# A decoder layer on one core: the context is split into two 16-bit parts first and transposed by DMA, instead of transposed on TensorE and split behind it

## What is computed

```python
src_trans = jnp.einsum('bsf,of->bso', src, W_src) + b_src       # src: the context, 8 x 512 x 1024
src_trans = src_trans * src_mask[:, :, None]
src_key, src_val = jnp.split(src_trans, 2, axis=2)              # keys and values of cross-attention
```

## Time and profile before

| | |
|---|---|
| median of three runs | 2157.06 us |
| the profiled execution, first to last instruction | 2153.7 us |
| TensorE busy | 1991.5 us (92%) |
| VectorE busy | 1472.0 us (68%) |
| ScalarE busy | 785.4 us (36%) |
| GpSimd busy | 179.0 us (8%) |
| context transposes on TensorE | 256 instructions, L567 |
| cT lo on VectorE | 64 instructions, 43.8 us |

### The profile page before, as it was taken

One profiled execution on the slowest core, in us unless ns is written; L12 is line 12 of the kernel. 1 busy time (PEld: TensorE's weight loads), 2 busy tenths in 40 slices (PEclk: granted clock), 3 DMA queues, 4 the chain that ended last, 5 costly groups with the idle time before them and its releaser, 6 DMA issues. The chain is left out here.

```text
span 2153.7 us, 35330 instructions
## 1 busy us (share of the span) xinstructions
PE 1991.5 (92%) x13100; PEld 1057.1 (49%) x13100; DVE 1472.0 (68%) x1762; ACT 785.4 (36%) x1209; POOL 179.0 (8%) x448
## 2 busy tenths in 40 slices
PE   6999898988899899956789999999999999999998
PEld 5555454544455445533454545545445454554543
DVE  4289997989898898898675556555565655656531
ACT  3322122122222122111574636536264462644622
POOL 0000002000010001053000010000100001000010
PEclk8999999999999899988899999999999999999999
DMA  6112221212111221312734041320413204141010
GB/s 207 40 50 59 74 65 49 69 60 64 64 59 58 70 74 50 110 52 83 179 111 104 2 95 50 64 80 1 100 44 81 64 1 109 35 95 30 1 40 20
DMA packets 151599, 143.35 MB, mean 67 GB/s; under 512 B 55529, under 2 KB 108777, under 8 KB 151426
## 3 DMA queue, kind: packets, MB, share of 16 engines
q1 hardware_dynamic: 147056, 140.58, 23.2%
q10 hardware_dynamic: 4370, 0.34, 0.2%
HBM read 94.75 MB, written 33.55 MB: 60 GB/s over the span
## 5 line engine op out<-in xcount | busy, mean ns | idle before, releaser
L1488 DVE TENSOR_TENSOR p_lo<-k,p_hi 128x1024 f16<-128x1024 f32 x128 | 156.8, 1225 | 193.8 <-ACT p_hi L1376 193.8
L888 DVE TENSOR_REDUCE ctx<-prod 128x512 f32<-128x4096 f32 (+1 forms) x32 | 215.3, 6728 | 0.1
L1177 PE MATMUL b_ff<-x2T_hi,w1T_hi 128*128 128x512 f16 x512 | 195.3, 381 | 2.3 <-DVE x2T_lo L1488 2.3
L1533 DVE CUSTOM_DVE_ANT_0 junk<-b_sx,mneg 128x512 f16<-128x512 f32 x256 | 175.7, 686 | 30.7 <-issue 22.3
L1177 PE MATMUL b_ff<-x2T_lo,w1T_hi 128*128 128x512 f16 x512 | 195.1, 381 | 0.0
L1177 PE MATMUL b_ff<-x2T_hi,w1T_lo 128*128 128x512 f16 x512 | 195.1, 381 | 0.0
L1408 ACT ACTIVATE k<-b_st,mbias 128x512 f32<-128x512 f32 x256 | 161.6, 684 | 14.2 <-PE b_st L1221 14.1
L604 PE MATMUL pj_b<-winT_hi,xT_hi 128*128 128x512 f16 x384 | 146.1, 380 | 6.3 <-DVE xT_lo L822 6.3
L1376 ACT ACTIVATE p_hi<-k 128x1024 f16<-128x1024 f32 x128 | 135.3, 1057 | 44.2 <-PE b_av L1236 41.9
L604 PE MATMUL pj_b<-winT_hi,xT_lo 128*128 128x512 f16 x384 | 145.5, 379 | 0.0
L604 PE MATMUL pj_b<-winT_lo,xT_hi 128*128 128x512 f16 x384 | 145.5, 379 | 0.0
(11 more groups left out here) (263 smaller groups left out, 4157.2 us busy)
## 6 DMA issues: line engine op xcount, KB each, us to landing
cn<-in_ctx_dram SPq DMA_DIRECT2D x64, 256.0 KB, 2.8
k<-kT_scratch SPq DMA_DIRECT2D x24, 512.0 KB, 7.9
xn<-in_x_dram SPq DMA_DIRECT2D x32, 256.0 KB, 2.9
xres<-in_x_dram SPq DMA_DIRECT2D x32, 256.0 KB, 3.0
x_scratch<-x SPq DMA_DIRECT2D x32, 256.0 KB, 2.0
q<-x_scratch SPq DMA_DIRECT2D x8, 1024.0 KB, 5.6
q<-x_scratch SPq DMA_DIRECT2D x32, 256.0 KB, 4.0
out_dram<-q SPq DMA_DIRECT2D x32, 256.0 KB, 4.5
```

What stands on the lines that cost most here:

```text
L888: dve.tensor_reduce(ctx1[:, cols], prod[:, :, cols].rearrange("p s e -> p e s"), AX.X, ALU.add).then_inc(s["av_done"], 1)
L1177: mm = pe.matmul(out, a, c, start=(start and n == 0), stop=end)
L1488: dve.tensor_tensor(dst, bank, hi, ALU.subtract).then_inc(out, 1)
L1533: dve.tensor_tensor_reduce(junk[:, :], sx_b[tt % 2][:, :], mneg[:, :], 1.0, NEG, ALU.add, ALU.max, mx[:, h % 2, tt:tt + 1]).then_inc(s["sx ...
```

## The change

The context quarter is split before it is transposed. ScalarE now copies the loaded rows `cn` to `cs_hi` (two buffers) in float16, GpSimd subtracts to get `cs_lo` (one buffer), and SyncE issues two DMA transposes, 128 x 512 float16 each, from these to cT hi and cT lo. TensorE's transposes of the context, the bank `st_b` and VectorE's `context_lo` are gone. Each of the two orders by hand keeps its places; the load of a quarter is issued one quarter earlier in the queue's count (off + 6 in place of off + 5), behind the two transposes of off + 4.

```diff
             def load_context(b, off):
-                wait_from(sp, s["st_filled"], 16 * b + off - 1)
+                wait_from(sp, s["c_lo"], 16 * b + off - 1)
...
+            def turn_context(b, off):
+
+                sp.wait_ge(s["c_lo"], 16 * b + off + 1)
+                stand_alone(sp, alone["sp"])
+                wait_from(sp, s["sm_filled"], 16 * b + off - off % 4 - 4)
+                stand_alone(sp, alone["sp"])
+                for z, src in enumerate((cs_hi[off % 2], cs_lo)):
+                    sp.dma_start_transpose(cT_part(z, off), src[:, :]).then_inc(c_turned[off % 2], 16)
...
             def s_phase(b, tail):                                  # SyncE
                 for t, offs in enumerate(S_QUARTERS):
                     for off in offs:
-                        load_context(b, off + 5)
+                        turn_context(b, off + 4)
+                        load_context(b, off + 6)
...
+            def context_lo(b, off):                                # GpSimd
+
+                pool.wait_ge(s["c_hi"], 16 * b + off + 1)
+                wait_from(pool, c_turned[(off - 1) % 2], 32 * (8 * b + (off + 1) // 2))
+                pool.tensor_tensor(cs_lo[:, :], cn[off % 2][:, :], cs_hi[off % 2][:, :],
+                                   ALU.subtract).then_inc(s["c_lo"], 1)
...
-            def context_transposes(b, off):                        # TensorE
-
-                wait_from(pe, s["st_lo"], 16 * b + off)
-                pe.wait_ge(cn_ld[off % 2], 16 * (8 * b + off // 2 + 1))
-                for j in range(4):
-                    mm = pe.transpose(st_b[:, j * P:(j + 1) * P], cn[off % 2][:, j * P:(j + 1) * P], w.ident[:, :])
-                mm.then_inc(s["st_filled"], 1)
...
                 if c == 0:                                         # TensorE, context_products
-                    pe.wait_ge(s["st_lo"], n + 4)
+                    for i in range(2):
+                        pe.wait_ge(c_turned[i], 64 * (4 * b + off // 4 + 1))
...
             def context_hi(b, off):                                # ScalarE
-                act.wait_ge(s["st_filled"], 16 * b + off + 1)
-                act.activation(cT_part(0, off), bank4(st_b), ACT.Copy).then_inc(s["st_hi"], 1)
+                act.wait_ge(cn_ld[off % 2], 16 * (8 * b + off // 2 + 1))
+                wait_from(act, c_turned[off % 2], 32 * (8 * b + off // 2))
+                act.activation(cs_hi[off % 2][:, :], cn[off % 2][:, :], ACT.Copy).then_inc(s["c_hi"], 1)
...
-            def context_lo(b, off):                                # VectorE
-                low(cT_part(1, off), bank4(st_b), cT_part(0, off), s["st_hi"], 16 * b + off + 1, s["st_lo"])
```

More of the change, by code:

```diff
@@ L313, in phase_a @@
     cn = [sb(f"cn{i}", [P, 512], F32) for i in range(2)]
+    cs_hi, cs_lo = [sb(f"cs_hi{i}", [P, 512], F16) for i in range(2)], sb("cs_lo", [P, 512], F16)
     cT = [pair(f"cT{i}", [P, CT, 256]) for i in range(2)]
@@ L372, in av_operands, with has_quarter @@
         return by_head(prod), probs, by_head(v)
-    def has_transposes(b, off):
-        return not (isinstance(b, int) and 16 * b + off + 4 >= QUARTERS)
+    def has_quarter(b, off):
+        return not (isinstance(b, int) and 16 * b + off >= QUARTERS)
     def bank4(bank):
@@ L456, in av_phase @@
                     for off in offs:
-                        if has_transposes(b, off + 1):
-                            load_context(b, off + 5)
+                        if has_quarter(b, off + 4):
+                            turn_context(b, off + 4)
+                        if has_quarter(b, off + 6):
+                            load_context(b, off + 6)
                     if t < T - 1:
@@ L463, in av_phase @@
                     for off in offs:
-                        if off % 4 == 2 and has_transposes(b, off - 2):
+                        if off % 4 == 2 and has_quarter(b, off + 2):
                             load_mask(b, off + 2)
@@ L477, in _ @@
                 load_x(0, t)
-            for off in range(2, 5):
-                load_context(0, off)
+            for off in range(4):
+                turn_context(0, off)
+                load_context(0, off + 2)
             s_phase(0, False)
@@ L537, in s_phase @@
                     for off in offs:
+                        context_lo(b, off + 4)
                         if off % 4 == 2:
@@ L551, in _ @@
             scale_mask(0, 0)
+            for off in range(4):
+                context_lo(0, off)
             s_phase(0, False)
@@ L763, in s_phase @@
                     for i, off in enumerate(offs):
[L764 to L765 removed]
+                        context_hi(b, off + 4)
                         if i == 0:
@@ L777, in av_phase @@
                     for off in offs:
-                        if has_transposes(b, off):
+                        if has_quarter(b, off + 4):
                             context_hi(b, off + 4)
@@ L919, in av_phase @@
                 last = isinstance(b, int) and b == NB - 1
-                def transposes_lo(t, offs):
-                    for off in offs:
-                        if has_transposes(b, off):
-                            context_lo(b, off + 4)
-                    if not last:
-                        x_lo(b + 1, t)
                 for t, offs in enumerate(AV_QUARTERS):
                     if t == 0:
-                        transposes_lo(0, offs)
+                        if not last:
+                            x_lo(b + 1, 0)
                         softmax(b)
                     context_products(b, t)
-                    if t < 2:
-                        transposes_lo(t + 1, AV_QUARTERS[t + 1])
-                    elif t > 2:
-                        transposes_lo(t, offs)
+                    if not last and t != 2:
+                        x_lo(b + 1, t + 1 if t < 2 else t)
                     if t >= 2:
```

17 lines of the change are left out of this document (3 added, 14 removed).

## The result

The changed kernel takes 2213.0 us (median of four runs, 2212.2 to 2219.0) against 2157.6 us for the kernel before in the same comparison: a ratio of 1.027, interval 1.025 to 1.029. It is slower by 55 us. The forecast was 2126.1 us, and the range of 2110 to 2200 doesn't hold the result.

A forecast was written before the change was run, and what follows sets the result against it. TensorE was taken to set the pace in the scores stages, VectorE or TensorE in the values stages. Span 2153.7 - 32.6 for the removal + 1.6 stall = 2122.7 us, 2126.1 with the 3.4 us around it; range 2110 to 2200.

The forecast's parts named there:

- The removal: Work taken off TensorE and VectorE in phase_a: 0.49 us a quarter where TensorE paces, 0.60 where VectorE does, 32.6 us.
- The window of 99 us: Stretch of the earlier trace taken as one scores stage, with TensorE busy for 96.5 us and VectorE for 84.7.
- The split: Gain by place: 2.0 us before the first stage, 19.6 scores stages, 4.4 and 5.4 values stages, 1.2 last block.
- The transposes' own time P: Time from issuing a pair of transposes on SyncE until both have landed: 3.6 to 15.8 us, taken as 4.8.
- slow transposes: Rival: long transposes make TensorE stand at a group's first product; middle 2175 us, far end 2225; chance 0.33.
- The subtraction on GpSimd: 64 subtractions moved to GpSimd, 1.5 us each and up to 5.9 beside a VectorE product, costed at nothing.
- The row of 4.28 us: Earlier GpSimd instruction on a single column, begun 0.16 us after a VectorE product of two SBUF operands; it ended with it.
- The cover named: On SyncE, a quarter's transposes must wait anyway for the previous quarter's stores, which wait for VectorE's sums; this hides GpSimd's subtraction.
- SyncE's queue: Loads standing behind the transposes on SyncE are used two quarters later, so their delay was given no cost.
- The first product of a group: TensorE's wait for all four context tiles; room 4.4, 8.4 and 7.4 us for off 4, 8, 12; stall 1.6 us.
- transposes that eat the gain: Rival: transposes of 9.2 to 10.0 us a pair, or VectorE waiting for GpSimd, cancel the gain; 2157 us, chance 0.09.
- row of 3.37 us: Earlier VectorE product begun while a GpSimd instruction ran, against 3.35 us for its group; cited against GpSimd holding up products.

The follow-up runs named there:

- e5_removal: The kernel before, without TensorE's transposes, ScalarE's copy and VectorE's subtraction of the context, and nothing in their place: 2127.0 us, ratio 0.986.
- e4_copies: The changed kernel with each DMA transpose replaced by a plain DMA copy of the same 128 KB: 2185.4 us, ratio 1.012 to the kernel before.
- e1_order: The changed kernel with GpSimd's context subtraction ahead of the normalisation factors in the scores stages: 2189.1 us, ratio 1.014 to the kernel before.
- e11_memset: e6_mask with GpSimd writing zeros in place of the subtraction, all waits and transposes kept: 2128.2 us, ratio 0.986 to the kernel before.
- e2_xload: The changed kernel with SyncE's x loads moved ahead of the transposes: 2179.7 us, ratio 1.011 to the kernel before.
- e3_both: The changed kernel with the edits of e1_order and e2_xload together: 2152.3 us, ratio 0.997 to the kernel before.
- e6_mask: e3_both with GpSimd scaling the mask one quarter later and SyncE loading it ahead of the transposes: 2147.7 us, ratio 0.996 to the kernel before.

## Why the prediction was wrong

**The removal: right.** 32.6 us forecast, 32 measured (e5_removal), and VectorE did not become the bound, but for the last values stage, which is 1.8 us longer (TensorE's wait for VectorE's sums there is 7.3 us, 1.1 before). The window of 99 us taken for the scores stage ends 4.5 us too early, which this sum doesn't use. The split was off: the four scores stages lost 27.7 us in all instead of 19.6, the values stages 6.0 instead of about 11, so that the total's fit to 1 us is partly luck.

**The transposes' own time P: right, a little high.** Forecast 4.8 us for a pair, from 3.6 to 15.8. Measured 1.25 for the first issue and 2.5 for the second's landing, 3.75 us in the median of the 64 pairs (8.1 at most). The rival "slow transposes", the only one that ended on the slower side, had the sign but not the mechanism: it needed a P above 9.6 us. The two prices that it turned on stand thus in the trace: landing takes 2.4 to 2.5 us, issuing 1.20 to 1.25 us where the earlier trace rows have 0.60 for a copy. The Trainium skill's Advanced Engine Details and Errata (X-Bar Transpose), by which a transposing DMA is as fast as a plain one, agrees with the trace nearly for the landing (2.5 against 2.3 us) and not for the issue. The estimate of 10.5 us from VectorE: DVE Perf Modes (The three transpose paths) is not borne out: the eight blocks of a pair took 3.75 us. P as defined also misses what a longer issue does to whatever stands behind it on SyncE, and that was worth 28 us in this order (e4_copies).

**The subtraction on GpSimd: right in size, wrong in its cover. This is the step that failed.** Forecast 1.5 us each, up to 5.9; measured 1.15 alone, 2.0 in the mean, up to 5.4. The row of 4.28 us in the earlier trace rows was read rightly, and the contention that it and the rule speak of is there. But the text asked only what stands *behind* the subtraction in GpSimd's order ("the factors are used two values steps later"). In the scores stages of the later blocks the factors stand *ahead* of it, and the very row shows in its bracket that GpSimd had waited 24.05 us for VectorE. The cover named, SyncE's stores that come no earlier, is no cover for a subtraction that begins 24 us after ScalarE's copy. Price: 24 us for the factors (e1_order). On top of it come 19.5 us for the subtraction as such (e11_memset; 0.5 us of writing is left in there), which the forecast had at nothing.

**SyncE's queue: the second step that failed.** "On SyncE the loads, which are used two quarters later" was the whole reckoning. It holds for the context's loads. The x loads stand in the same queue, and TensorE takes them at the start of a values stage. They now stand behind transposes that wait for GpSimd, and behind the loop's end, and came 3.4 to 8.9 us late in six places. Price: 33 us (e2_xload). The rival "transposes that eat the gain" looked at VectorE instead: its product with q and k takes 4.47 us in the mean, against 4.41 before. The prediction's ground for this, that GpSimd gives way, was half of the truth: its row of 3.37 us had an overlap of 0.15 us only, and two products that began 0.04 us behind a subtraction took 5.39 us. They were few, so it cost little.

**The first product of a group.** The stall was made of P less the room between SyncE's place and the product. The room was read rightly, but it is room only if the transposes are issued when SyncE reaches that place. They were issued when GpSimd had delivered: 12.4 us of wait at the second group, where 0.4 were forecast. With the order mended and the subtraction short (e11_memset) it is 1.0.

**The clock: no term at all.** The prediction counts waits alone. Where TensorE stood, its granted clock fell, from 0.97 to 0.88 in the scores stage, and the work behind the wait ran at the lower level. By the estimate above that is some 22 of the 94 us between e5_removal and the changed kernel in `phase_a`; the prices of 24, 33 and 19.5 us hold their share of it. No run changed the clock by itself.

**The sum.** In the measured terms: 2158.9 - 32 for the removal, + 61 for the two orders (24 and 33 singly), + 25 for what e3_both keeps above e5_removal, is 2213. It closes by construction, since the terms are differences of the runs in a chain. Of the 25 us some 5 belong to the mask's place (e6_mask) and most of the others to the subtraction (e11_memset).

**What stays open.** `phase_a` ends 61 us later but the span is only 57 us longer, so `phase_b` is 4 us shorter after the change; no run was spent on it. A second `cs_lo`, a split of the 19.5 us, and the mask's place by itself in the last block weren't tried.

## What to carry to other kernels

When work is moved to another in-order queue, read three things for it: what stands ahead of it there and what that waits for, what stands behind it, and when its inputs are ready. Idle share (GpSimd busy for 11% of a stage) says nothing about the moment at which an engine is free; the bracket of the row ahead does. A step that several queues pass on (ScalarE, GpSimd, SyncE, DMA, TensorE) is only as early as the latest queue's position, and every urgent load behind it in the issuing queue inherits its waits. Where TensorE is the pace, price a wait at more than its length, because here the granted clock fell with it and the work behind it ran slower.

## What the hardware showed

- In the contention of GpSimd with VectorE the one that began first kept its time, and it depends on what GpSimd's instruction reads. A subtraction with two SBUF inputs takes 1.15 us alone and up to 5.4 us when it begins inside a product of two SBUF operands of VectorE, ending 1.0 us after the product's end (19 of 19 in the changed kernel). When it began 0.04 us ahead of the product, it took 1.16 us and the product 5.39 instead of 4.42. Beside VectorE's sums, which read one operand, it took 1.16 us. A memset of the same tile took 524 to 526 ns in all 64 cases.
- A DMA transpose of 128 x 512 float16 within SBUF lands in 2.4 to 2.5 us in the median, a copy in 2.3; but it occupies SyncE for 1.20 to 1.25 us instead of 0.60 to 0.63. With 128 of them that was worth 28 us in one order and 7 in another.
- TensorE stood for 12.4 us, and its granted clock was at 1.2 GHz for 13.7 us around this, 5 us of work among them; products of 128 x 256 started 0.21 us apart there and 0.11 behind it.
- Behind two loads of 3 MB together (and four stores) the issue of a transpose took up to 3.4 us.
